# Two-layer cross attention on one core: the row maxima go into the query stack by three transfers of one row each

## The chip, the cores and the metric

The kernel runs on one core of a Trainium2 chip. The metric is the device time of one execution in microseconds (us), given as the median of several runs; before the change it is 413.09 us.

## The reference

Two layers of the same grouped-query cross attention are applied one after the other to `x` (16 batches, 128 rows, 256 columns), each with its own weights and the same context `ctx_2048`:

```python
q = hidden_state @ Wq + bq          # 32 heads of 8
k = encoder_hidden_state @ Wk + bk  # 8 key heads of 8, each for 4 query heads
v = encoder_hidden_state @ Wv + bv
scores = einsum('bkgld,bksd->bkgls', q, k) * 8**-0.5 + mask
attn = softmax(scores, axis=-1)
out = einsum('bkgls,bksd->bkgld', attn, v)   # back to (batch, 128, 256)
x = out @ Wo + bo + hidden_state
return (x - mean(x)) * rsqrt(var(x) + 1e-6) * gamma + beta
```

All values are float32. The mask of these inputs is zero everywhere.

## The kernel before

The work is cut into 32 units (`UNITS`): 16 batches of layer 0 and then 16 of layer 1. Each engine runs a list of phases; phase t holds work of several units at once: scores of unit t, the softmax and the values of units t-1 and t-2, the end of units t-3 and t-4, and the projections of unit t+2. `walk` (L85) writes some phases out one by one and puts the phases 5 to 12 and 21 to 28 into loops of four phases a turn. Within each engine the order is the order of the source; semaphores tie the engines together.

Scores are computed twice. Each float32 query and key is split into three bf16 parts (`PARTS` = 3), and the products of parts stand as rows of two stacks in SBUF: `q_stack` and `k_stack`, four buffers each (`RING`), with rows 0 to 71 for the products of parts (padded with zeros to 96). First `scores` (L655) makes the scores with queries on the partitions, one bank of four heads at a time, and the VectorE takes the maximum of each row (`maximum`, L520). Then `scoresT` (L675) makes them again, transposed, from 99 rows of the stacks: rows 96 to 98 of `q_stack` hold the negated row maxima in three bf16 parts, and the same rows of `k_stack` hold ones, so that the maximum is subtracted inside the matmul and ScalarE can take the exponential at once (L436).

How the maxima get there: after the eighth `maximum` of unit u, `copy_max` (L527) repeats the 32 maxima of each query three times, TensorE transposes them (`transpose_max`, L731 to L740) into 96 partitions, and in the next phase the VectorE splits them with four instructions in `max_rows` (L533; L539, L541, L544, L546) into `max_parts`: partitions 0 to 31 hold the third part of the 32 heads, 32 to 63 the second, 64 to 95 the first, 128 bf16 values (256 bytes) in each partition. `max_parts` has two buffers. The transfer of L290 then copies these 96 rows of 256 bytes into the partitions 96 to 98 of `q_stack`, 32 rows behind each other in each partition. It counts up `max_rows_loaded` by 16. Three places wait on that semaphore: the SyncE queue itself, before it issues the transfer of the next unit (L288); `max_rows` (L538), before it writes over the buffer of two units before; and `scoresT` of the first key head (L678), which is TensorE's to wait for.

In TensorE's list of phase t (L793 to L850), the first `scoresT` of unit t-1 comes after the fifth bank of scores of unit t (L829 to L832). Behind it in the same queue stand the rest of the scores of unit t, the projections and the products with the values.

All transfers are issued by SyncE (L251 to L348), in one queue, in this order in a phase: the maxima of unit t-1 (L290), y of unit t-4 to the result or back to `x_sb` (L298, L301), in layer 0 the inputs of unit t+3 (L258, two) and x of unit t (L312), the query parts of unit t+2 to DRAM (L318), in layer 0 its key parts (L322, three, one for each part), and, when these have landed, the loads of the two stacks of unit t+2 from DRAM (L332 for `q_stack`, L338 for `k_stack`).

Of the kernel before, what the change touches and what calls it, by code (L numbers as in the profile page):

```python
# [37 lines left out]
HEADS, KV, HD = 32, 8, 8  # L38
# [3 lines left out]
PARTS = 3  # L42
TERM_ROWS = PARTS * PARTS * HD
SCORE_ROWS = 96
MAX_ROW = 96
STACK_ROWS = MAX_ROW + PARTS
RING = 4
# [26 lines left out]
def need(engine, sem, count):  # L74

    if not isinstance(count, int) or count > 0:
        engine.wait_ge(sem, count)
# [22 lines left out]
def cross_attention(nc, x, xT, ctxT, mask, w_q, w_kv, w_o, b_q, b_k, rows, out):  # L100
    with ExitStack() as ctx:
        def sb(name, shape, dt):
            return ctx.enter_context(nc.sbuf_tensor(name, shape, dt))
# [36 lines left out]
        q_stack = sb("q_stack", [P, RING, HEADS, L], BF16)  # L140
# [3 lines left out]
        max_parts = sb("max_parts", [PARTS * HEADS, 2, L], BF16)  # L144
# [63 lines left out]
        max_rows_loaded = sem("max_rows_loaded")  # L208
# [19 lines left out]
        MAXT_STEPS, NORM_STEPS, MASK_STEPS = 4, 5, 5  # L228
# [22 lines left out]
        @block.sync  # L251
        def _(sp):
            xT_d = xT.rearrange("(k p) b l -> p k b l", p=P)

            def load_inputs(b, slot, loaded):
                for to, from_ in ((xT_sb[:, :, b], xT_d[:, :, b]),
                                  (ctx_sb[:, slot], ctxT[b].rearrange("(k p) s -> p k s", p=P))):
                    sp.dma_start(to, from_).then_inc(loaded, 16)  # L258


            STARTERS = 2
            sp.dma_start(wq_sb[:, 0], w_q[0].rearrange("(k p) n -> p k n", p=P)).then_inc(weights_loaded, 16)
            load_inputs(0, 0, weights_loaded)
            sp.dma_start(wkv_sb[:].rearrange("p k a n -> p k (a n)"),
                         w_kv.rearrange("(k p) n -> p k n", p=P)).then_inc(weights_loaded, 16)
            sp.dma_start(bq_sb[:], b_q).then_inc(biases_loaded, 16)
            sp.dma_start(bk_sb[:], b_k).then_inc(biases_loaded, 16)
            load_inputs(1, 1, inputs_loaded)
            sp.dma_start(rows_sb[:].rearrange("p a n -> p (a n)"), rows.partition_broadcast(P)).then_inc(rows_loaded, 16)
            sp.dma_start(mask_sb[:], mask.rearrange("b o l s -> l (b o) s")).then_inc(all_masks_loaded, 16)  # L270

            def phase(turn, step, loop_layer):
                t, r = turn + step, step % RING

                def of(per, k):

                    return turn * per + per * (step + k)

                if not isinstance(turn, int):

                    for count in (of(MAXT_STEPS, 0), of(16, -1), of(KV, -RING), of(3, 3), of(1, 0),
                                  of(16 * INPUT_DMAS, 2), of(16, 0), of(2, -3), of(16, -4), of(1, -3),
                                  of(16 * STACK_DMAS, 2), of(16, 3), of(16 * PARTS, 3), of(KV, 3 - RING)):
                        sp.to_reg(count)
                if live(t - 1):

                    need(sp, maxT_step, of(MAXT_STEPS, 0))
                    need(sp, max_rows_loaded, of(16, -1))  # L288
                    need(sp, scoresT_ready, of(KV, -RING))
                    sp.dma_start(q_stack[MAX_ROW:MAX_ROW + PARTS, (r - 1) % RING],  # L290
                                 max_parts[:, (r - 1) % 2].rearrange("p (o l) -> p o l", o=1)).then_inc(max_rows_loaded, 16)
                u, ru = t - 4, r
                if live(u):
                    layer, b = place(u, loop_layer)
                    need(sp, affine_step, of(2, -3))
                    need(sp, y_left, of(16, -4))
                    if layer == LAYERS - 1:
                        sp.dma_start(out[b], y[:, ru % 2]).then_inc(y_left, 16)  # L298
                    else:
                        need(sp, x_bo_ready, of(1, -3))  # L300
                        sp.dma_start(x_sb[:, b], y[:, ru % 2]).then_inc(y_left, 16)  # L301
                layer, b = place(t + 3, loop_layer)
                if (not isinstance(t, int) or t + 3 >= STARTERS) and layer == 0:

                    need(sp, qk_projected, of(1, 0))
                    need(sp, v_projected, of(1, 0))
                    need(sp, inputs_loaded, of(16 * INPUT_DMAS, 2))
                    load_inputs(b, (r + 3) % RING, inputs_loaded)
                layer, b = place(t, loop_layer)
                if live(t) and layer == 0:  # L310
                    need(sp, x_loaded, of(16, 0))
                    sp.dma_start(x_sb[:, b], x[b]).then_inc(x_loaded, 16)  # L312
                u, ru = t + 2, (r + 2) % RING
                layer, b = place(u, loop_layer)
                if live(u):

                    need(sp, q_split, of(3, 3))
                    sp.dma_start(q_scratch[u].rearrange("a p n -> p a n"), q_parts[:, ru % 2]).then_inc(q_stored, 16)  # L318
                    if layer == 0:
                        need(sp, k_split, of(3, 3))  # L320
                        for part in range(PARTS):
                            sp.dma_start(k_scratch[b, :, :, part].rearrange("a d (h s) -> (a d) h s", h=KV),  # L322
                                         k_parts[:, ru % 2, part]).then_inc(k_stored, 16)

                    need(sp, stacks_loaded, of(16 * STACK_DMAS, 2))

                    need(sp, scoresT_ready, of(KV, 3 - RING))
                    if isinstance(u, int) and u < RING:
                        need(sp, k_padded, 1)
                        need(sp, q_padded, u + 1)  # L330
                    need(sp, q_stored, of(16, 3))
                    sp.dma_start(q_stack[0:TERM_ROWS, ru].rearrange("p h l -> p (h l)"),  # L332
                                 q_scratch[u].rearrange("a (d h) n -> (a d) (h n)", d=HD).unsqueeze(1)
                                 .broadcast_to([PARTS * HD, PARTS, HEADS * L])
                                 ).then_inc(stacks_loaded, 16)
                    if layer == 0:
                        need(sp, k_stored, of(16 * PARTS, 3))
                    sp.dma_start(k_stack[0:TERM_ROWS, ru].rearrange("p h l -> p (h l)"),  # L338
                                 k_scratch[b, layer].rearrange("d a n -> (d a) n").partition_broadcast(PARTS)
                                 ).then_inc(stacks_loaded, 16)  # L340
                if isinstance(t, int) and t == 0:
                    sp.dma_start(wo_sb[:], w_o.rearrange("a (k p) n -> p a k n", p=P)).then_inc(later_weights_loaded, 16)
                    sp.dma_start(wq_sb[:, 1], w_q[1].rearrange("(k p) n -> p k n", p=P)).then_inc(later_weights_loaded, 16)

            walk(sp, phase)
            sp.wait_ge(y_left, 16 * UNITS)
            sp.wait_ge(q_stored, 16 * UNITS)
            sp.wait_ge(k_stored, 16 * PARTS * BATCH)  # L348
# [151 lines left out]
        def _(dve):  # L500
# [32 lines left out]
            def max_rows(u, ru):  # L533


                m, parts = misc_bank[0:PARTS * HEADS, 0:L], max_parts[:, ru % 2]
                need(dve, maxT_ready, u + 1)
                need(dve, max_rows_loaded, 16 * (u - 1))  # L538
                nc.vector.tensor_scalar(parts, m, -1.0, None, ALU.mult).then_inc(maxT_step, 1)  # L539
                dve.wait_ge(maxT_step, MAXT_STEPS * u + 1)  # L540
                nc.vector.scalar_tensor_tensor(out=max_rest[:], in0=m, scalar=-1.0, in1=parts,  # L541
                                               op0=ALU.mult, op1=ALU.subtract).then_inc(maxT_step, 1)
                dve.wait_ge(maxT_step, MAXT_STEPS * u + 2)
                nc.vector.tensor_copy(parts[0:2 * HEADS], max_rest[0:2 * HEADS]).then_inc(maxT_step, 1)  # L544
                dve.wait_ge(maxT_step, MAXT_STEPS * u + 3)
                nc.vector.tensor_tensor(parts[0:HEADS], max_rest[0:HEADS], parts[0:HEADS], ALU.subtract  # L546
                                        ).then_inc(maxT_step, 1)
# [106 lines left out]
        def _(pe):  # L654
# [20 lines left out]
            def scoresT(u, ru, kv, masked):  # L675

                if kv == 0:
                    need(pe, max_rows_loaded, 16 * (u + 1))  # L678
                need(pe, exp_done, KV * u + kv - 1)
                mm = nc.tensor.matmul(t_bank[kv % 2][:], k_stack[0:STACK_ROWS, ru, kv],  # L680
                                      q_stack[0:STACK_ROWS, ru, GROUP * kv:GROUP * (kv + 1)],
# [217 lines left out]
```

## Time and profile before

| what | us |
|---|---|
| median of 3 runs | 413.09 |
| the runs | 409.84, 413.18, 413.09 |
| span of the profiled execution | 413.5 |
| TensorE busy | 332.6 |
| VectorE busy | 303.6 |
| GpSimd busy | 249.6 |
| ScalarE busy | 237.1 |

The profiled execution's own time is its span, 413.5 us from its first to its last instruction; it lies 0.4 us above the median of the runs. Busy times are those of the profile; register, semaphore and DMA-issuing instructions are not counted as busy. In the rows below PE is TensorE (PEld its weight loads), DVE VectorE, ACT ScalarE, POOL GpSimd and SPq the queue of SyncE, where the duration of a row is that of the issuing instruction and not of the transfer. Over the whole span the granted clock of TensorE is 0.915 of the full one on average.

### The profile page before, as it was taken

How to read it: one execution, taken by the hardware profiler on the slowest of the kernel's cores; microseconds unless marked ns; L12 is line 12 of the kernel's file. 1: busy time of each engine (PE TensorE's matmuls, PEld its weight loads, DVE VectorE, ACT ScalarE, POOL GpSimd, SP SyncE). 2: the span in 40 equal slices, each digit the busy share in tenths (PEclk: the TensorE clock that was granted, in tenths of full speed). 3: DMA queues.
4: the chain of work that ended last, by engine and by line, in shares of the span. 5: the costliest groups of instructions: out<-in, count | busy, mean ns of one | idle time of the engine just before them, and what ended most of it. 6: DMA issues, size and time to landing. Idle time of an engine off the chain costs nothing.

```text
span 413.5 us, 10069 instructions
## 1 busy us (share of the span) xinstructions
PE 332.6 (80%) x2688; PEld 220.3 (53%) x2688; DVE 303.6 (73%) x796; ACT 237.1 (57%) x530; POOL 249.6 (60%) x505
## 2 busy tenths in 40 slices
PE   3371478898799798979989888988888988888982
PEld 3361355665566564756646555555555655544431
DVE  4432347787669586867969899989989999997832
ACT  2210146677467475756757777766656766654760
POOL 8046505676568576666757766666666766664234
PEclk9855569999889898998989999999999999998997
DMA  7715744544635445453434333333333333331000
GB/s 203 196 35 148 177 112 131 141 131 122 154 88 152 130 131 143 124 151 95 123 108 119 106 109 105 97 116 104 100 113 106 105 110 107 105 93 35 15 29 25
DMA packets 45928, 46.44 MB, mean 112 GB/s; under 512 B 12736, under 2 KB 40640, under 8 KB 43584
## 3 DMA queue, kind: packets, MB, share of 16 engines
q1 hardware_dynamic: 45888, 45.96, 39.8%
q8 instruction: 19, 0.31, 0.3%
q14 instruction: 21, 0.17, 0.1%
HBM read 33.10 MB, written 9.96 MB: 104 GB/s over the span
## 4 chain that ended last, share of the span: by engine, by line
PE 35%; DMA 28%; DVE 18%; issue 11%; POOL 3%; SPq 2%; DVEq 1%; POOLq 0%
DMA q_stack<-max_parts 24%; PE oT_bank L748 9%; PE t_bank L680 8%; PE s_bank L665 8%; DVE row_max L523 5%; PE qk_bank L722 3%; DVE max_parts L546 3%; DVE max_parts L544 3%; PE o_bank L761 2%; DMA mask_sb<-mask 2%; DVE max_rest L541 2%; DMA q_scratch<-q_parts 2%; PE misc_bank L700 2%; DVE max_parts L539 2%; DVE v_ones L603 1%
## 5 line engine op out<-in xcount | busy, mean ns | idle before, releaser
L523 DVE TENSOR_REDUCE row_max<-s_bank 128x4 f32<-128x512 f32 x256 | 171.5, 681 | 68.7 <-PE s_bank L665 67.5
L436 ACT ACTIVATE probs<-t_bank 128x512 f32<-128x512 f32 x256 | 148.7, 602 | 86.7 <-PE t_bank L680 86.5
L680 PE MATMUL t_bank<-q_stack,k_stack 99*128 99x512 bf16 x256 | 102.2, 400 | 44.0 <-DMA q_stack<-max_parts 43.9
L665 PEld LDWEIGHTS s_bank<-k_stack,q_stack 96*128 96x128 bf16 x1024 | 77.4, 103 | 92.2 <-issue 44.5
L665 PE MATMUL s_bank<-k_stack,q_stack 96*128 96x128 bf16 x1024 | 106.2, 230 | 19.7 <-DMA k_stack<-k_scratch 16.5
L748 PE MATMUL oT_bank<-probs,v_ones 128*32 128x512 f32 x512 | 72.7, 642 | 0.2 <-ACT probs L436 0.2
L393 POOL TENSOR_TENSOR scaled<-normed,rows_sb 128x256 f32<-128x256 f32 x32 | 23.2, 726 | 52.8 <-DVE normed L584 52.8
L680 PEld LDWEIGHTS t_bank<-q_stack,k_stack 99*128 99x128 bf16 x256 | 25.7, 101 | 52.2 <-DMA q_stack<-max_parts 44.2
L452 ACT ACTIVATE qT<-qk_bank,bq_scaled 128x128 f32<-128x128 f32 x64 | 23.4, 366 | 49.4 <-PE qk_bank L727 29.3
L441 ACT ACTIVATE oT_sb<-oT_bank 128x512 f32<-128x512 f32 x64 | 39.1, 610 | 18.7 <-PE oT_bank L748 18.7
L236 POOL TENSOR_TENSOR q_rest<-qT,q_parts 128x256 f32<-128x256 f32 x31 | 20.9, 675 | 42.9 <-ACT q_parts L452 33.5
L389 POOL TENSOR_TENSOR rstd<-var_eps,minus_half 128x1 f32<-128x1 f32 x32 | 17.6, 550 | 45.4 <-DVE var_eps L580 44.8
L722 PE MATMUL qk_bank<-xT_sb,wq_sb 128*128 128x128 f32 (+1 forms) x256 | 38.2, 297 | 7.5 <-DMA wkv_sb<-w_kv 6.2
L722 PEld LDWEIGHTS qk_bank<-xT_sb,wq_sb 128*128 128x128 f32 x256 | 37.1, 211 | 9.2 <-issue 7.0
L761 PE MATMUL o_bank<-identf,oT_sb 128*128 128x128 f32 x256 | 39.4, 277 | 1.0 <-ACT oT_sb L441 0.9
L761 PEld LDWEIGHTS o_bank<-identf,oT_sb 128*128 128x128 f32 x256 | 32.1, 144 | 7.9 <-ACT oT_sb L441 2.7
L780 PE MATMUL misc_bank<-wo_sb,attnT 128*128 128x256 f32 x128 | 33.0, 379 | 0.5 <-ACT attnT L466 0.5
L780 PEld LDWEIGHTS misc_bank<-wo_sb,attnT 128*128 128x128 f32 x128 | 24.2, 190 | 3.3 <-ACT attnT L466 0.7
L400 POOL TENSOR_TENSOR y<-scaled,rows_sb 128x256 f32<-128x256 f32 x32 | 23.2, 726 | 3.6 <-POOL scaled L393 1.4
L452 ACT ACTIVATE q_parts<-qk_bank,bq_scaled 128x128 bf16<-128x128 f32 x64 | 23.4, 366 | 0.0
L424 POOL TENSOR_TENSOR x_bo<-x_sb,rows_sb 128x256 f32<-128x256 f32 x32 | 23.4, 731 | 0.0
L239 POOL TENSOR_TENSOR q_parts<-q_rest,q_parts 128x256 bf16<-128x256 f32 x31 | 20.8, 672 | 2.4
(67 smaller groups left out, 432.6 us busy)
## 6 DMA issues: line engine op xcount, KB each, us to landing
q_stack<-q_scratch SPq DMA_DIRECT2D x32, 576.0 KB
q_scratch<-q_parts SPq DMA_DIRECT2D x32, 192.0 KB, 2.5
k_stack<-k_scratch SPq DMA_DIRECT2D x32, 144.0 KB
xT_sb<-xT SPq DMA_DIRECT2D x16, 128.0 KB, 2.8
ctx_sb<-ctxT SPq DMA_DIRECT2D x16, 128.0 KB, 3.4
x_sb<-x SPq DMA_DIRECT2D x16, 128.0 KB, 2.5
x_sb<-y SPq DMA_DIRECT2D x16, 128.0 KB, 2.5
result<-y SPq DMA_DIRECT2D x16, 128.0 KB, 2.3
```

The costliest lines, as they stand in the source:

```text
L393: nc.gpsimd.tensor_tensor(scaled[:], normed[:], rows_sb[:, layer, D:2 * D], ALU.mult).then_inc(affine_step, 1)
L424: nc.gpsimd.tensor_tensor(x_bo[:], x_sb[:, b], rows_sb[:, layer, 0:D], ALU.add).then_inc(x_bo_ready, 1)
L436: nc.scalar.activation(probs[:, ru % 2, kv], t_bank[kv % 2][:], ACT.Exp).then_inc(exp_done, 1)
L441: nc.scalar.activation(oT_sb[:, half], oT_bank[:], ACT.Copy).then_inc(oT_copied, 1)
L452: nc.scalar.activation(q, qk_bank[:, k * L:(k + 1) * L], ACT.Identity, bias=bq_scaled[:, place(u, layer)[0], k:k + 1], scale=SCALE).then_i ...
L523: nc.vector.tensor_reduce(row_max[:, ru % 2, GROUP * kv:GROUP * (kv + 1)], s_bank[kv % 2][:].rearrange("p (g s) -> p g s", g=GROUP), AX.X, ...
L665: mm = nc.tensor.matmul(s_bank[kv % 2][:, g * S:(g + 1) * S], q_stack[0:SCORE_ROWS, ru, GROUP * kv + g], k_stack[0:SCORE_ROWS, ru, kv], st ...
L680: mm = nc.tensor.matmul(t_bank[kv % 2][:], k_stack[0:STACK_ROWS, ru, kv], q_stack[0:STACK_ROWS, ru, GROUP * kv:GROUP * (kv + 1)], start=Tr ...
L722: mm = nc.tensor.matmul(qk_bank[:, n * L:(n + 1) * L], wq_sb[:, layer, k, n * P:(n + 1) * P], xT_sb[:, k, b], start=(n == 0 and k == 0), s ...
L748: mm = nc.tensor.matmul(oT_bank[32 * j:32 * (j + 1)], v_ones[:, ru, kv], probs[:, ru % 2, kv], start=True, stop=True)
L761: mm = nc.tensor.transpose(o_bank[:, g * P:(g + 1) * P], oT_sb[:, half, g * L:(g + 1) * L], identf[:])
L780: mm = nc.tensor.matmul(misc_bank[:, 0:D], attnT[:, k], wo_sb[:, layer, k], start=(k == 0), stop=(k == KT - 1))
```

## The change

The one transfer of L290 becomes three, each from 32 partitions of `max_parts` into one partition of `q_stack`. All three count up the same semaphore, and each count that is waited for becomes three times as large.

```diff
-                    need(sp, max_rows_loaded, of(16, -1))
+                    need(sp, max_rows_loaded, of(16 * PARTS, -1))
                     need(sp, scoresT_ready, of(KV, -RING))
-                    sp.dma_start(q_stack[MAX_ROW:MAX_ROW + PARTS, (r - 1) % RING],
-                                 max_parts[:, (r - 1) % 2].rearrange("p (o l) -> p o l", o=1)).then_inc(max_rows_loaded, 16)
+                    for part in range(PARTS):
+                        sp.dma_start(q_stack[MAX_ROW + part:MAX_ROW + part + 1, (r - 1) % RING],
+                                     max_parts[HEADS * part:HEADS * (part + 1), (r - 1) % 2]).then_inc(max_rows_loaded, 16)
...
-                need(dve, max_rows_loaded, 16 * (u - 1))
+                need(dve, max_rows_loaded, 16 * PARTS * (u - 1))
...
-                    need(pe, max_rows_loaded, 16 * (u + 1))
+                    need(pe, max_rows_loaded, 16 * PARTS * (u + 1))
```

The same factor stands in the list of counts that SyncE puts into registers at the start of each turn of a loop (L281).

## Rows read from the trace of the kernel before

**Rows 1.** The page, part 4: shares of the span in the chain that ended last
```profile
PE 35%; DMA 28%; DVE 18%; issue 11%; POOL 3%; SPq 2%; DVEq 1%; POOLq 0%
```

**Rows 2.** Waits of the whole span, the engines', then SyncE's: us, times, longest
```profile
PE t_bank L680 <- DMA q_stack<-max_parts: 43.9, 28, 6.9
...
SPq L290 <- DVE max_parts L546: 116.3, 31, 7.5
```

**Rows 3.** The chain in order of time, one phase of layer 1: start, us, what
```profile
236.27 0.67 DVE max_parts L546
...
236.96 3.02 DMA q_stack<-max_parts
...
240.03 0.39 PE t_bank L680
...
247.39 3.01 DMA q_stack<-max_parts
```

**Rows 4.** The chain in order of time, other transfers of the maxima
```profile
106.26 5.18 DMA q_stack<-max_parts
...
131.60 4.85 DMA q_stack<-max_parts
145.05 3.42 DMA q_stack<-max_parts
...
179.51 5.51 DMA q_stack<-max_parts
...
279.17 2.83 DMA q_stack<-max_parts
...
372.21 3.87 DMA q_stack<-max_parts
```

**Rows 5.** Timeline of SyncE's queue, a phase of layer 0: start, us of issue
```profile
121.27 0.77 SPq L290 DMA_DIRECT2D q_stack<-max_parts  x1
...
124.91 0.39 SPq L318 DMA_DIRECT2D q_scratch<-q_parts  x1
...
128.95 0.78 SPq L338 DMA_DIRECT2D k_stack<-k_scratch  x1
131.60 0.77 SPq L290 DMA_DIRECT2D q_stack<-max_parts  x1
```

**Rows 6.** The same queue, three issues in a row in an unrolled phase, and layer 1
```profile
87.85 1.89 SPq L322 DMA_DIRECT2D k_scratch<-k_parts  x3
...
241.71 0.74 SPq L338 DMA_DIRECT2D k_stack<-k_scratch  x1
```

**Rows 7.** Issuing instructions by tile: ns least/median/most, first and last start
```profile
L290 SPq DMA_DIRECT2D q_stack<-max_parts x32: 727/760/790, 45.2 to 391.8; - x32
...
L322 SPq DMA_DIRECT2D k_scratch<-k_parts x48: 546/598/1581, 12.4 to 198.6; - x48
...
L312 SPq DMA_DIRECT2D x_sb<-x x16: 354/409/1582, 34.8 to 217.7; - x16
```

**Rows 8.** DMA issues by line: KB each, median us from issue to landing
```profile
x_sb<-y SPq DMA_DIRECT2D x16, 128.0 KB, 2.5
...
k_scratch<-k_parts SPq DMA_DIRECT2D x48, 32.0 KB, 2.0
```

**Rows 9.** Stretches: us, busy by engine, granted clock, share of 16 DMA engines, GB/s
```profile
238.20:238.35 0.15, 0.15 (x4) 0.15 (x2) 0.15 (x1) 0.11 (x1) 0.01 (x1) 1.00 0.00 0
238.35:238.85 0.50, 0.50 (x8) 0.49 (x7) 0.50 (x2) 0.48 (x1) 0.00 (x0) 1.00 0.21 47
...
239.05:239.50 0.45, 0.03 (x1) 0.00 (x0) 0.45 (x5) 0.23 (x1) 0.00 (x0) 1.00 0.88 280
...
156.80:158.20 1.40, 1.40 (x14) 1.20 (x13) 1.27 (x3) 1.40 (x4) 1.32 (x3) 1.00 0.19 69
```

**Rows 10.** Stretches, same columns: behind a late transfer, and layer 1
```profile
111.40:121.20 9.80, 9.71 (x65) 6.15 (x65) 4.93 (x15) 4.64 (x11) 4.49 (x10) 0.68 0.39 105
...
240.00:250.00 10.00, 9.34 (x81) 6.03 (x81) 9.00 (x22) 7.25 (x16) 7.02 (x14) 1.00 0.35 101
```

More of the change, by code:

```diff
@@ L279, in phase @@
                 if not isinstance(turn, int):
-                    for count in (of(MAXT_STEPS, 0), of(16, -1), of(KV, -RING), of(3, 3), of(1, 0),
+                    for count in (of(MAXT_STEPS, 0), of(16 * PARTS, -1), of(KV, -RING), of(3, 3), of(1, 0),
                                   of(16 * INPUT_DMAS, 2), of(16, 0), of(2, -3), of(16, -4), of(1, -3),
```

## The prediction

> **What bounds the kernel now.** I read the chain that ended last first. DMA holds 28% of it [rows 1], and nearly all of that is one transfer, the one that the change cuts up. In order of time the chain has 26 pieces of it that sum to 99.2 us, 24% of the span [rows 3, 4]. A phase of layer 1 shows the loop: VectorE's last split of the maxima (L546) ends at 236.94, the transfer takes 3.02 us, TensorE starts L680 at 240.03, and 7.41 us after the landing the next transfer is issued at 247.39 [rows 3]. Behind the one of 4.85 us issued at 131.60 the same distance is 8.60, up to 145.05 [rows 4]. So a period is the latency of this transfer plus 7.4 us or somewhat more, and a microsecond added to or taken from the latency should come out whole in the time. The waits confirm it from the other side: TensorE waits for this transfer 28 times, 43.9 us in all, and SyncE waits for L546 before it issues 31 times [rows 2]: the queue is nearly always ready before the data.
>
> The latency has two kinds. Of the 26 pieces 13 last over 3.4 us (8.66 for the first unit, then up to 5.51, mostly in layer 0), 13 last 2.83 to 3.28; the six that the chain doesn't hold I count as quiet. So there are 19 quiet ones and 13 held up. What holds them up: the loads of the stacks. In layer 0 the load of `k_stack` is issued 7.68 us after L290 and only 2.65 us before the next L290, whose transfer then takes 4.85 us; in layer 1 it is issued 5.68 us before the next (241.71 to 247.39), which takes 3.01 [rows 3 to 6].
>
> **The quiet latency, term by term.** Only a small part of the 3.02 us is data. Issued at 236.96, the transfer moves nothing up to 238.35 (no DMA work in the stretch before that), then 0.5 us at a share of 0.21, some three of 16 engines, and 47 GB/s x 0.5 us = 24 KB, all of it; a further 1.1 us passes until TensorE goes on [rows 9]. Spreading the data can save at most that half microsecond.
> What is added is issue time. The issue of L290 takes 0.76 us [rows 7]; it is followed by two more. No row shows a 32-row transfer from SBUF into one partition. The nearest for pitch is L322, 128 rows of 256 bytes in a rearranged pattern, three in a row: 1.89 us for three of 0.60, a pitch of (1.89 - 0.60) / 2 = 0.645 us [rows 6, 7]. The lower bound is a plain 0.41 us issue (L312) with 0.05 between, 0.46; the upper is L290's own 0.76 with 0.05, 0.81. I take 0.65, since L322 has the size of row and the reshaping in common.
> From the issue of the last one to its landing: L322 with 32 KB takes 2.0 us, x_sb<-y with 128 KB 2.5 [rows 8]. With 8 KB I take 2.0; the ends are 1.75 (2.0 less half of the data time seen above) and 2.5.
> Latency after: 2 x 0.645 + 2.0 = 3.29 us, against 2.98 as the mean of the quiet pieces now (99.2 less the 60.4 of the held-up ones, over 13): +0.31. From both sides: 2 x 0.46 + 1.75 = 2.67 (-0.31), and 2 x 0.81 + 2.5 = 4.12 (+1.1). 19 x 0.31 = +5.9 us.
>
> **The held-up ones.** Two things pull against each other. Everything behind L290 in SyncE's queue is issued later: three issues of 0.60 and two gaps of 0.05 in place of 0.76 make +1.14 us. In layer 0 the queue runs from L290 to the load of `k_stack` nearly without a gap [rows 5], so that load comes 1.14 us later, and what it still has to move lies that much longer ahead of the next maxima. Against this, the load drains at a share of 0.19, again three engines [rows 9]; if each new transfer is spread over all 16, the three loaded engines have 6 rows of 256 bytes to do behind it in place of 32, which saves about the 0.5 us of data time. The next L290 itself is 0.31 us later by the quiet term. 1.14 - 0.31 - 0.5 = +0.3 a piece. The bounds: +1.1 as for the quiet ones, and -1.0, if the rows now wait behind more than the data time shows. 13 x 0.3 = +3.9 us.
>
> The rest costs nothing while it has cover. The waits of L538 and L288 are for landings of one or two units before, a phase of 10 us away. What the queue delays (y, the inputs, the query parts) is needed a phase or more later. SyncE's last issue ends 1.87 us before the next L290 in a short phase of layer 0 (128.95 + 0.78 to 131.60, register work among it [rows 5]); +1.14 fits, while at the upper pitch +1.6 (3 x 0.76 + 0.10 - 0.76) would leave next to nothing.
>
> Sum: 413.5 + 5.9 + 3.9 = 423.3 us for the profiled execution; the median of the runs is 0.4 below its span, so 422.9, rounded 423.0.
>
> **Two rules of the Trainium skill.** The stretch of 0.5 us shows three engines at work on L290, while x_sb<-y runs at a share of 0.88 [rows 9]. DMA: Bandwidth & Descriptors, in the section on why a DMA increments its semaphore by 16, says that the slowest dimension other than 1 on both sides sets the number of engines; the new shape has 32 on the side of the source in place of 3 against 96, so by that rule all 16 take part. The trace agrees for the old shape. On the other hand the same page's rules for kernel authors say to coalesce many small transfers, since under 64 KB one pays mostly overhead; here 24 KB becomes three times 8 KB. The trace agrees there too: 2.5 of the 3.02 us are not data. By the first rule alone the latency would fall by up to 0.5 us a unit, to about 397 us; by the second it rises.
>
> **The rivals.**
> *Spreading wins (faster).* Place: the landing of L290 behind the load of `k_stack`, on the same three engines. The excess of the 13 held-up ones over 2.98 us is 21.7 us in all. If that excess were mostly these rows being interleaved with other traffic on three engines, then with six rows there it would shrink by two thirds, -14.5 us; with the +5.9 of the quiet ones that gives 404. It decides from a saving of 0.5 us a held-up unit on (5.9 / 13). For it: the second transfer's rows arrive late anyway, so that the added issue time is hidden while the engines drain. Against it: the three engines show 0.19 without a break up to 158.2, which is the load itself, and the new rows wait for that as well, with the load now later. Chance 0.14.
> *It cancels (no change).* A pitch near 0.46 gives 2 x 0.46 + 2.0 = 2.92 quiet, much as now, and the held-up ones gain and lose alike: 413. For it: plain issues take 0.41 us. Against it: these patterns aren't plain, and L290's takes 0.76. Chance 0.13.
> *The issue is dear, or the clock goes (slower still).* At a pitch of 0.81 and 2.2 us to land the quiet latency is 3.8: 19 x 0.82 + 13 x 0.5 = +22, 435 us. Close to it: TensorE waits some 1.1 us a phase in layer 1 at a granted clock of 1.00 (2.4 GHz); behind the transfer of 5.18 us the clock is 0.68 on average, a mix of that level and 1.2 GHz, and the next issue comes 9.8 us after the landing in place of 7.4 (106.26 + 5.18 to 121.27) [rows 4, 5, 10]. Two or three more phases like this are within the range; one in each phase would be more. Chance 0.2.
> My forecast has the rest, 0.53.
>
> **How the numbers follow.** 423.0 us is the likeliest case, with 417 to 430 as its own range (pitch 0.55 to 0.72). The range of all goes from 407, where quiet ones stay and the held-up ones gain 0.5 us each, to 436. About 1% is what a measurement of this kernel can tell from no change. Faster by over 1% is the first rival: 0.14; within 1% the second and a little of the forecast: 0.15; slower: 0.71.
>
> **What would show it.** Right: three issues in a row at a pitch of 0.6 to 0.7 us in SyncE's timeline, quiet pieces of the chain from the first issue to TensorE's start of 3.2 to 3.4 us, a distance from the landing to the next issue still at 7.4, the load of `k_stack` some 1.1 us later behind L290, and held-up ones of 4 to 5.5 us as before. Wrong: chain pieces under 2.9 us in layer 1 (then issue or landing is cheaper than its nearest rows), held-up pieces gone or below 3.6 (then the three engines were the brake), or a period that doesn't follow the latency.

## The result, and the profile after

| | before | after |
|---|---|---|
| median of the runs, us | 413.13 (4 runs, 409.84 to 413.76) | 422.96 (4 runs, 420.10 to 425.33) |
| span of the profiled execution, us | 413.5 | 421.4 |
| ratio after to before | | 1.027, 95% interval 1.0195 to 1.0345 |

The change makes the kernel slower: the medians differ by 9.8 us, 2.4%, and the ratio above, which is formed from the runs and not from the medians, says 2.7%. Executions over 1.5% longer than the fastest of their kernel are left out of every ratio and interval in this document, but not out of the medians. 423.0 was forecast, with 417 to 430 as the likeliest case's own range.

First the chain that ended last, after, as shares of the span. It answers to [rows 1].

```profile
PE 33%; DMA 22%; DVE 19%; issue 11%; SPq 11%; POOL 3%; DVEq 1%; POOLq 0%
```

SyncE's queue, 2% of the chain before, now holds 11%, and DMA went from 28% to 22%. The same piece of work is the brake, but a part of it is now issue time. One phase of layer 1 in order of time (start us, us, what), which answers to [rows 3]:

```profile
250.08 0.67 DVE max_parts L547
...
250.76 0.57 SPq L291
...
251.37 0.59 SPq L291
...
252.00 1.92 DMA q_stack<-max_parts
...
253.96 0.39 PE t_bank L681
...
261.33 0.57 SPq L291
```

The first issue comes right behind VectorE's last split, the second 0.61 us later, the third at 252.00, 1.24 us behind the first, and 1.92 us later all has landed. That is 3.16 us in place of 3.02 in the phase of [rows 3], and from the landing at 253.92 to the next issue at 261.33 it is 7.41 us, exactly the distance of before. The page's table of issues and the tile's durations give the two terms over all 96 transfers (KB each and median us to landing; then ns least/median/most):

```profile
q_stack<-max_parts SPq DMA_DIRECT2D x96, 8.0 KB, 2.0
...
L291 SPq DMA_DIRECT2D q_stack<-max_parts x96: 502/587/1531, 44.3 to 400.0; - x96
```

The held-up transfers are still there. Of this chain, pieces that begin with the third issue; the timeline of SyncE beside them shows the queue of one phase of layer 0, which answers to [rows 5]:

```profile
146.45 3.74 DMA q_stack<-max_parts
...
170.68 3.65 DMA q_stack<-max_parts
...
197.01 2.88 DMA q_stack<-max_parts
```

```profile
121.84 1.86 SPq L291 DMA_DIRECT2D q_stack<-max_parts  x3
...
131.31 0.78 SPq L339 DMA_DIRECT2D k_stack<-k_scratch  x1
133.08 2.81 SPq L291 DMA_DIRECT2D q_stack<-max_parts  x3
```

The load of `k_stack` goes out 9.47 us behind the first issue of the maxima, where it was 7.68: 1.8 us later, of which 1.1 are the two added issues; the rest are short waits in between. Over the phases of layer 0 the median of that distance is 8.6 in place of 7.5, just those 1.1. It stands 1.77 us in front of the next maxima, where it was 2.65. In the last row the three issues take 2.81 us in place of 1.86; that is taken up below.

How many engines take part can be read from the number of packets on the page (before, then after):

```profile
q1 hardware_dynamic: 45888, 45.96, 39.8%
```

```profile
q1 hardware_dynamic: 47328, 45.96, 39.0%
```

1440 more for 32 units is 45 a unit. In the trace's DMA records of this queue only the packets of 4 bytes became more, from 3392 to 4832. I read them as the packets with which each engine that takes part counts up the semaphore. Then they rose from 3 to 48 a unit, if the old transfer used three engines (its share of 0.21 in [rows 9] says so), 16 for each new one. The trace's updates of `max_rows_loaded` bear it out: after, DMA updated it 1536 times, 16 times for each of the 96 transfers.

**Where the 7.9 us between the two profiled executions come from.** I take a unit's latency from its first issue to its last landing, and the rest of the period up to the next first issue. In both executions 19 of the 32 are quiet (below 3.4 us) and 13 held up.

| term, us | before | after | difference |
|---|---|---|---|
| up to the first issue | 45.2 | 44.3 | -1.0 |
| 19 quiet latencies | 56.6 | 60.0 | +3.4 |
| 13 held-up latencies | 60.5 | 62.4 | +1.9 |
| from landing to next issue, 31 times | 232.6 | 235.2 | +2.7 |
| behind the last landing | 18.6 | 19.5 | +0.9 |

The fourth row is no constant. Behind a late landing TensorE has stood idle and its granted clock is lower for a while, as the rows below show; the distance was over 8 us five times before and is so seven times after. One stretch behind a late landing and one behind a quiet one, after (columns as in [rows 9]); they answer to [rows 10]:

```profile
174.40:184.20 9.80, 9.80 (x65) 6.27 (x65) 4.90 (x14) 4.60 (x10) 4.50 (x10) 0.67 0.46 125
208.00:217.00 9.00, 8.95 (x85) 6.09 (x81) 8.15 (x23) 7.10 (x17) 5.76 (x11) 1.00 0.27 86
```

In the first the granted clock is 0.67 on average, a mix of the two levels 2.4 and 1.2 GHz, and the next issue comes 10.0 us behind the landing in place of 7.4.

### The profile page after: what moved, and what is told of

It is laid out like the page before. It is cut to its first block, busy times and chain, and to the rows that moved or that the text cites. A ratio compares the mean times of both kernels' runs of the same rounds, so it can differ in the third digit from the quotient of the medians.

```text
span 421.4 us, 10139 instructions
## 1 busy us (share of the span) xinstructions
PE 333.2 (79%) x2688; PEld 219.6 (52%) x2688; DVE 303.0 (72%) x796; ACT 237.2 (56%) x530; POOL 250.1 (59%) x505
## 4 chain that ended last, share of the span: by engine, by line
PE 33%; DMA 22%; DVE 19%; issue 11%; SPq 11%; POOL 3%; DVEq 1%; POOLq 0%
DMA q_stack<-max_parts 18%; SPq L291 9%; PE t_bank L681 8%; PE oT_bank L749 8%; PE s_bank L666 7%; PE qk_bank L723 4%; DVE row_max L524 4%; DVE max_parts L547 3%; DVE max_parts L545 3%; DVE max_rest L542 2%; DMA mask_sb<-mask 2%; PE o_bank L762 2%; DVE max_parts L540 2%; PE misc_bank L701 2%; DMA ctx_sb<-ctxT 1%
## 5 line engine op out<-in xcount | busy, mean ns | idle before, releaser
L681 PE MATMUL t_bank<-q_stack,k_stack 99*128 99x512 bf16 x256 | 103.1, 404 | 48.3 <-DMA q_stack<-max_parts 48.1
L442 ACT ACTIVATE oT_sb<-oT_bank 128x512 f32<-128x512 f32 x64 | 39.1, 611 | 19.1 <-PE oT_bank L749 19.1
L781 PE MATMUL misc_bank<-wo_sb,attnT 128*128 128x256 f32 x128 | 33.9, 387 | 0.5 <-ACT attnT L467 0.5
```

What stands on the lines that cost most here:

```text
L442: nc.scalar.activation(oT_sb[:, half], oT_bank[:], ACT.Copy).then_inc(oT_copied, 1)
L781: mm = nc.tensor.matmul(misc_bank[:, 0:D], attnT[:, k], wo_sb[:, layer, k], start=(k == 0), stop=(k == KT - 1))
```

## The experiments

The theory: a unit's latency is the pitch of the issues in front of the last one plus the last one's landing, and a second loss comes through SyncE's queue, because what stands behind the maxima in it, the load of `k_stack` above all, goes out later and then holds up the next maxima. The rivals: the number of transfers or their spread over all engines costs something by itself; or the loss is only one of the two terms. In the table, "layer 0" is the time from the first issue of the maxima of unit 0 to that of unit 16, "layer 1" from unit 16 to unit 31, both in the profiled execution.

| kernel | median us | before beside it | ratio (95%) | layer 0 | layer 1 |
|---|---|---|---|---|---|
| before | 413.13 | | | 191.7 | 154.8 |
| after | 422.96 | 413.13 | 1.027 (1.0195 to 1.0345) | 195.9 | 158.6 |
| e1_staged | 403.47 | 412.17 | 0.980 (0.973 to 0.987) | 186.0 | 149.3 |
| e2_two | 416.28 | 412.17 | 1.008 (1.004 to 1.0125) | | |
| e3_extra | 436.01 | 412.17 | 1.063 (1.055 to 1.072) | 202.2 | 161.2 |
| e4_kspread | 401.81 | 412.17 | 0.976 (0.969 to 0.983) | 182.1 | 151.9 |
| e5_after_kspread | 413.97 | 410.72 | 1.007 (1.001 to 1.013) | 188.1 | 154.6 |
| e6_staged_kspread | 389.08 | 410.72 | 0.950 (0.9405 to 0.960) | 176.3 | 147.4 |
| e7_staged_two_kspread | 392.12 | 410.72 | 0.959 (0.952 to 0.9665) | 182.6 | 142.4 |
| e8_x_once | 395.60 | 410.44 | 0.9595 (0.949 to 0.970) | | |
| e9_after_x_once | 415.58 | 410.44 | 1.0135 (1.005 to 1.022) | | |

The kernel before was run again beside each group of kernels, and its own median lay between 410.4 and 413.1 us; kernels of different rows are best set against each other by their ratios. The profiled executions of e2, e8 and e9 were the longest of their kernels (421.4, 397.4 and 421.5 us), so their stretches are left out. That of e5 was the shortest of its ten (408.5 us) and that of e3 the shortest of its four (432.5 us).

### e1_staged: each transfer as soon as its part is split

```diff
-                    need(sp, maxT_step, of(MAXT_STEPS, 0))
...
-                    for part in range(PARTS):
+                    for part, left in ((2, 3), (1, 1), (0, 0)):
+                        need(sp, maxT_step, of(MAXT_STEPS, 0) - left)
```

(Left out: the list of the counts that SyncE puts into registers.)

> Three transfers as in the change, but each issued as soon as its own part is split: the first part after L539, the second after L544, the third after L546. Theory (latency = pitch of the issues + landing of the last one; the engines and the number of transfers cost nothing by themselves): only one issue and one landing lie behind L546, 1.92 us in place of 3.16, so quiet periods fall from 10.57 to the 9.3 to 9.6 us at which VectorE is full; held-up ones stay. Time 395 to 403 us. Rival (what costs is the number of transfers, their wide spread over the engines and the semaphore counts): no less than 418 us, the latency behind L546 stays near 3 us.

403.5 us, 19.5 below the change and 8.7 below the kernel before, with the same 96 transfers over the same 16 engines. The rival falls: three wide transfers are not slow by themselves, what counts is how much of them stands behind the last split. The time lies just above what was expected (395 to 403), and the landing is the likely reason. The tile's summary line (least/median/most of all landings, from each issue) of e1:

```profile
DMA to landing us min/median/max: 1.8/2.4/6.8
```

and of the changed kernel:

```profile
DMA to landing us min/median/max: 1.8/2.0/6.5
```

The median landing is 2.4 in place of 2.0. As the periods shrink, the load of `k_stack` lies nearer to the next maxima, also in layer 1: it is issued 2.9 us before them in the median there, where it was 4.6 in the changed kernel. The expectation that "held-up ones stay" was too simple, more transfers of the maxima became held up. That this load does it here too fits the rows, but no run shows it by itself. TensorE still waits 33.4 us in all for the maxima, against 48.1 after and 43.9 before.

### e2_two: two transfers in place of three

```diff
-                    for part in range(PARTS):
-                        sp.dma_start(q_stack[MAX_ROW + part:MAX_ROW + part + 1, (r - 1) % RING],
-                                     max_parts[HEADS * part:HEADS * (part + 1), (r - 1) % 2]).then_inc(max_rows_loaded, 16)
+                    for first, last in ((1, 3), (0, 1)):
+                        sp.dma_start(q_stack[MAX_ROW + first:MAX_ROW + last, (r - 1) % RING],
+                                     max_parts[HEADS * first:HEADS * last, (r - 1) % 2].rearrange("p (o l) -> p o l", o=1)
+                                     ).then_inc(max_rows_loaded, 16)
```

(Against the changed kernel; the counts, 32 in place of 48, follow and are left out.)

> Two transfers in place of three: 64 rows into two partitions, then 32 rows into one. Theory (pitch + landing of the last): the second is issued 0.65 to 0.8 us after the first and lands 1.92 us later, 2.6 to 2.75; the first, on two engines with 32 rows each, lands about as the transfer of before, 2.8 to 2.9, so that quiet latencies are 2.85, as before, and the time is 411 to 415 us. Rival (each transfer more costs its share, half of what the change cost): 418 us.

416.3 us, between the two. The time alone can't tell them apart: the interval of its ratio puts it 1.7 to 5.2 us above the kernel before, and half of the change's price is 4.9. Its chain in layer 1 has the quiet latency that the theory gave:

```profile
338.49 0.70 SPq L291
339.24 2.06 DMA q_stack<-max_parts
```

2.81 us from the first issue to the landing, no more than before. So the 3 to 4 us that are left are not in the quiet latency. They fit a queue that is 0.6 us longer (issues of 0.70 and 0.59 in place of 0.76), the term that my expectation for this kernel had left out; that they come from there is argued and not shown. In the profiled execution the 19 quiet latencies sum to 54.3 us (before 56.6) and the 13 held-up ones to 66.2 (before 60.5), which has the sign of that reading, but it is the longest execution of ten.

### e3_extra: the queue made longer, the transfer of the maxima left alone

```diff
+                    need(sp, spare_loaded, of(32, -1))
+                    for n in range(2):
+                        sp.dma_start(spare[MAX_ROW + n:MAX_ROW + n + 1], ident[HEADS * n:HEADS * (n + 1)]
+                                     ).then_inc(spare_loaded, 16)
```

(Left out: the tile `spare` and its semaphore, a wait for `ident` at the start of SyncE's list and one for the last of these transfers at its end.)

> The kernel before with its one transfer, and behind it in SyncE's queue two more of 8 KB for which nobody in the phase waits (from a constant into a spare tile, same shape as in the change; this is work beyond the reference's). Theory (the second term of the prediction: what is queued behind goes out 1.25 us later, so the load of k_stack holds up the next maxima for longer): quiet latencies stay at 2.8 to 3.0 us, the held-up ones of layer 0 grow by 0.6 to 1.2 us each, time 419 to 426 us. Rival (the queue behind L290 has room, all of the loss is the pitch in front of the last landing): 411 to 415 us.

436.0 us, +24, where 419 to 426 was expected: the direction is the theory's, the size is twice its. Nobody in a phase waits for these two transfers, yet they cost more than the whole change. The chain shows both kinds of latency grown, held-up ones in layer 0 and now also in layer 1:

```profile
121.53 6.13 DMA q_stack<-max_parts
146.96 6.40 DMA q_stack<-max_parts
...
302.11 4.54 DMA q_stack<-max_parts
...
335.72 3.21 DMA q_stack<-max_parts
346.43 3.16 DMA q_stack<-max_parts
```

Over its 32 units the latencies sum to 133.9 us, against 117.1 before and 122.4 after. Sixteen are held up, by 5.17 us on average (before 13, 4.65; after 13, 4.80), and the quiet ones are mostly at 3.16, 0.2 to 0.3 above before, which I had not expected. That part is not the theory's: 0.32 us more (3.16 against 2.84) in each of 32 units would be some 10 of the 16.8 us by which the latencies grew (an estimate), and a quiet unit is one that the load of `k_stack` doesn't hold up. Only the other 6.6 us or so are left for that load.

Set beside the change this is the most telling run. The load of `k_stack` goes out equally late behind the first issue, 9.50 us here and 9.47 there:

```profile
121.53 0.76 SPq L292 DMA_DIRECT2D q_stack<-max_parts  x1
...
131.03 0.78 SPq L344 DMA_DIRECT2D k_stack<-k_scratch  x1
```

But here the maxima travel as one transfer on three engines and there as three on sixteen. The change is 13 us faster than e3. A quiet unit takes 3.16 us in both, so the 11.5 us between the two sums of latencies (133.9 and 122.4) lie with the held-up ones: the narrow transfer suffers more from what runs beside it. How e3's +24 us divides between the later load and the two extra transfers, which also carry data, isn't shown; for that a run would have to lengthen the queue without adding a transfer.

### e4_kspread: the load of k_stack in three transfers

```diff
-                    sp.dma_start(k_stack[0:TERM_ROWS, ru].rearrange("p h l -> p (h l)"),
-                                 k_scratch[b, layer].rearrange("d a n -> (d a) n").partition_broadcast(PARTS)
-                                 ).then_inc(stacks_loaded, 16)
+                    for n in range(PARTS):
+                        sp.dma_start(k_stack[TERM_ROWS // PARTS * n:TERM_ROWS // PARTS * (n + 1), ru].rearrange("p h l -> p (h l)"),
+                                     k_scratch[b, layer].rearrange("d a n -> (d a) n")).then_inc(stacks_loaded, 16)
```

(with `STACK_DMAS = 4`)

> The kernel before, with the load of k_stack made of three transfers of 24 rows each, which by the shape can use twelve engines in place of three. Theory (what holds the maxima up is this load on the three engines that also carry them): its data drain in about a fourth of the time, the held-up latencies fall from 3.4 to 5.5 us to below 3.5 in most units although SyncE issues 1.3 us more per phase, time 396 to 405 us. Rival (what holds them up is SyncE's late issue or the traffic of all loads together): held-up latencies stay above 4 us in layer 0, time 410 to 420 us.

401.8 us, as expected, and the rival falls: only six latencies are over 3.4 us, in place of 13. The same kind of edit as the change, one transfer made three, here wins 10 us. Its packets and its issues show why:

```profile
q1 hardware_dynamic: 46944, 45.96, 43.1%
```

```profile
L339 SPq DMA_DIRECT2D k_stack<-k_scratch x96: 313/356/1348, 16.7 to 354.4; - x96
```

1056 packets more are 33 a unit, from 3 to 36: twelve engines for each transfer. And the three issues take 0.36 us each, 1.2 us together, against 0.75 for the one: the split costs the queue only 0.45 us, not the 1.3 that was expected. A quiet landing stays at 2.87 in layer 1.

### e5_after_kspread: the change on top of e4

> The changed kernel with the load of k_stack in three transfers of 24 rows, as in e4_kspread; to be set against e4_kspread (401.8 us). With the held-up latencies mostly gone, the change's own price is left. Theory (pitch in front of the last landing, and room in SyncE's queue): quiet latencies 3.15 us in place of 2.87 in layer 1, +0.3 a unit, and in layer 0 the queue, which was busy for some 9.4 us a phase, is busy for 10.5 and begins to set the period: 409 to 415 us. Rival (what the change cost came only through the load of k_stack on three engines): 401 to 404 us, as e4_kspread.

414.0 us, 12.2 above e4_kspread; the rival falls. The size is less certain than the sign: the ten runs lie between 408.5 and 417.9 us, but even the lowest is above all four of e4 (at most 402.3), and by the two ratios to the kernel before, 1.007 and 0.976, the change costs 3% here. The price of the change is not tied to the slow load: with it mended, quiet latencies in layer 1 are 3.13 in place of 2.87, and eleven latencies are over 3.4 us again, in place of six, ten of them in layer 0; all latencies sum to 117.2 us, against 107.0 in e4. The room in SyncE's queue has shrunk as well:

```profile
SPq L291 <- DVE max_parts L547: 76.2, 29, 6.7
```

SyncE waits 76 us in all for the last split, where it waited 100 in the changed kernel and 116 before [rows 2].

### e6_staged_kspread and e7_staged_two_kspread: both together

e6 has the edits of e1 and of e4; e7 sends 64 rows after L544 (of the kernel before) and 32 after L546.

> Both at once: each of the three transfers as soon as its part is split (e1_staged), and the load of k_stack in three (e4_kspread). Theory (the two took different things away: the pitch and a part of the landing from in front of TensorE, and the drain of three engines): the gains add where SyncE has room. Layer 1: latency behind the last split 1.92 us and periods of 9.3 to 9.6, VectorE full; layer 0: SyncE is busy for some 10.5 us a phase and sets the period. Time 385 to 394 us. Rival (one of the two gains only moved the wait, so that they don't add): 398 to 403 us.

> As e6_staged_kspread, but with two transfers of the maxima: 64 rows into two partitions after L544, and the last 32 rows after L546. One issue less per phase, 0.6 us. Theory (in layer 0 SyncE's queue is the bound): layer 0 gains up to 0.6 us a phase against e6_staged_kspread, layer 1 loses 0.1 to 0.3 us a phase because 64 rows on two engines land 2.85 us after L544: 383 to 392 us, within 4 us of e6_staged_kspread. Rival (the queue isn't the bound): slower than e6_staged_kspread by 3 us or more.

e6 takes 389.1 us, 5.0% below the kernel before: the gains add (8.7 + 10.4 = 19.1 expected from e1 and e4, 21.6 measured). This version beats both the kernel before and the change. e7 is 3.0 us slower, at the point where its expectation drew the line, so it tells little: in layer 0, where it has one issue less, it is slower (182.6 against 176.3), in layer 1 faster (142.4 against 147.4), the opposite of what I had reckoned. That SyncE's issues alone bound layer 0 of e6 is thus not borne out.

### e8_x_once and e9_after_x_once: one issue less in layer 0

```diff
-                    need(sp, x_loaded, of(16, 0))
-                    sp.dma_start(x_sb[:, b], x[b]).then_inc(x_loaded, 16)
...
+                    sp.dma_start(x_sb[:], x.rearrange("b p d -> p b d")).then_inc(x_loaded, 16)
```

(The new line stands in phase 0; GpSimd's wait for x, left out, becomes one for 16.) e8 is e6 with this edit, e9 the changed kernel with it.

> As e6_staged_kspread, and the 16 loads of x in layer 0 are made one load of 2 MB in phase 0: SyncE issues one transfer less in each phase of layer 0, with its register work 0.55 us. Theory (in layer 0 SyncE's queue sets the period, or how late the load of k_stack goes out): layer 0 gains 0.3 to 0.55 us a phase, 5 to 8 us, against 389.1 us, less what the 2 MB cost at the start: 381 to 387 us. Rival (the queue has room, and layer 0 is bound by its transfers): 388 to 392 us.

> The changed kernel with the same one load of x: its queue in layer 0 is shorter by 0.55 us a phase, half of the 1.04 us that the change added (1.86 in place of 0.77 and the gap). Theory (the length of the queue in front of the load of k_stack is a large part of the loss, as e3_extra said): the load goes out 0.5 us earlier and the held-up latencies of layer 0 fall by 0.3 to 0.5 us: 415 to 420 us. Rival (the pitch in front of the landing is all): 422 to 424 us.

e8 missed: 395.6 us, 6.5 above e6 and outside what theory and rival gave. e9 came out as the theory has it: 415.6 us, 7.4 below the change, though only 4.7 when each is set against the kernel before beside it (+5.1 and +9.8), and the intervals of the two ratios overlap. In the trace of each the load of all of x delays the start, the first issue of the maxima comes at 47.6 us (e6: 42.2) and at 50.1 (after: 44.3). Behind that point e9's trace is 7.4 us shorter in layer 0, where the queue has half a microsecond less per phase, and 0.7 longer in layer 1, where it has the same. e8's trace is only 2.0 us shorter than e6's in layer 0, which doesn't pay for the start, and 4.5 longer in layer 1, which no edit explains; the traces of e8 and e9 are each of the longest execution. In e8 the load of `k_stack` is spread, in e9 not, and one could read from this that a long queue is dear only while it pushes a load on three engines against the maxima. That is not shown, and e5 speaks against it: there the load is spread as well, and the longer queue with the later landing still cost 3%.

## Why the prediction was right, by its own steps

**What bounds the kernel: right.** That a microsecond of latency comes out whole is shown in the chain after (7.41 us again between landing and next issue) and by e3's trace: its latencies sum to 16.8 us more than before, the distances from landing to next issue to the same 232.6, and its span is 17.1 us longer. e1, which takes time from behind the last split, gets 19.5 us back against the change. Behind late landings more than the latency is lost, see below.

**The pitch: right.** 0.645 was taken from L322; it is 0.62, issues of 0.587 us and a gap of 0.03 to 0.04. Neither the plain issue of 0.41 nor the old one of 0.76 would have done.

**The landing: right, slightly too long.** 2.0 was taken, 1.92 measured. Latency after: 3.29 forecast, 3.16 measured; against 2.98 that is +0.18 a quiet unit and +3.4 us in all, where the sum had +5.9.

**The held-up ones: the net has the right sign, its terms are not confirmed.** +3.9 forecast, +1.9 in the two traces. It is the difference of two terms of opposite sign. What spreading gives back, put at 0.5 us a held-up unit or 6.5 us in all, is larger: against e3, with the queue equally long and the quiet latency the same, the held-up units of the change have 11.5 us less. The queue term, +1.14 - 0.31 a unit or +10.8 in all, stands in no run by itself. e3's +24 us is more than it, but the two transfers also made every quiet landing later, which the term doesn't hold. A third term, the late issues and landings beside instruction packets (last section), was not foreseen and holds up to some 5 us of the 62.4.

So the near hit of 423.0 is in part luck, and a reader should take it for less than it looks. In the traces the two terms of the sum came to +5.3 us in place of +9.8, and terms that weren't in the sum brought the difference up to 7.9. The likeliest case's own range was also not what its words say: with the rest of the sum worked out in the same way, pitches of 0.55 and 0.72 give some 418 and 427, not 417 and 430.

**The distance from landing to next issue: left out of the sum.** It was named in the third rival (two or three more phases behind a lower clock "are within the range"); the traces have two more such phases, and +2.7 us.

**From the profiled execution to the median: wrong in form.** I set the execution's own time equal to its span, 0.4 us above the median. Later runs list both numbers, for instance 423.27 us with a span of 421.4, so 1.9 us lie around the span. The profiled execution of before thus took an estimated 415.4 us, and was 2 us slower than its median; its own time is not on record. That accounts for the 1.9 us between the traces' difference of 7.9 and the medians' of 9.8; executions of one kernel differ by 4 to 5 us here.

**The rivals.** "Spreading wins" had a true mechanism, as e4 and the change beside e3 show, but not the size to turn the sign. "It cancels" asked for a pitch of 0.46. "The issue is dear, or the clock goes" was half there: the issue wasn't dear, the clock went twice more.

**The two rules of the Trainium skill.** The rule on the number of engines in DMA: Bandwidth & Descriptors, in the section on why a DMA increments its semaphore by 16, gave the right counts: by the packets 3 before and 16 after, and 12 for e4's 24 rows. As a forecast of the time it would by itself have had the wrong sign here and the right one for e4. The same page's rule for kernel authors to coalesce many small transfers would have had the right sign here and the wrong one for e4.

Which way a split goes could be estimated from the rows: whether the data time on few engines (0.5 us for 24 KB; some 2 us for the load of 144 KB at the 69 GB/s of its stretch [rows 9]) is larger than the issues that the split adds.

## What to carry to other kernels

Cut a transfer into several only where its data time on few engines is longer than the added issues, or where the parts are ready at different times and each can leave at once; on the way to a waiting engine, what was issued before the last producer was done came nearly free here (e1). When SyncE issues everything in one queue, cost each added transfer also by what it pushes towards the next critical one, and by what it does beside the critical one: two transfers a phase that nobody waited for cost 24 us here, in shares that stay open. And look at the outermost dimension of the transfers that run beside the critical one: an ordinary-looking broadcast load on three engines cost 10 us (e4).

## What the runs showed of the hardware that I had not expected

**Issues that hang for a microsecond.** Four issues of the maxima take 1.37 to 1.53 us after, in place of 0.59. None of the maxima's did before, when the longest was 0.79, though one of L322 and one of L312 took 1.58 [rows 7]. In the chain:

```profile
133.08 0.60 SPq L291
...
133.72 1.53 SPq L291
...
135.30 2.38 DMA q_stack<-max_parts
```

Two units of layer 1, which the table above counts with the held-up ones (4.10 and 4.11 us), land a microsecond late without a long issue of their own. Here is one of them, behind an ordinary unit:

```profile
283.79 1.92 DMA q_stack<-max_parts
...
294.46 2.85 DMA q_stack<-max_parts
```

and the next issue in the queue takes 1.17 us in place of 0.4:

```profile
295.31 1.17 SPq L299 DMA_DIRECT2D result<-y  x1
```

All six stand beside a packet of the instruction queue. In the trace's DMA records a packet of 16,384 bytes lasts 0.98 us from 86.1 on, 1.36 from 133.5, 1.25 from 195.3, 1.22 from 218.7, 1.08 from 295.0 and 1.21 from 370.5; the long issues begin at 86.1, 133.7, 195.5, 218.9, 295.3 and 370.7. The long issue of L322 in the trace before (1.58 us at 100.5) stands beside such a packet too (100.4). The page before has 19 of these packets, as many as after:

```profile
q8 instruction: 19, 0.31, 0.3%
```

The likely reading is that a transfer on all sixteen engines, in a queue that is busy with the maxima for 1.86 us a phase in place of 0.76, meets such a packet more often than one on three. For it: an issue of the maxima takes over 1 us three or four times in the trace of each kernel with three transfers on sixteen engines (after, e1, e5, e6, e8, e9), and never in the others. Against the width alone: e2 and e7 have one such transfer a phase and e3 has two, and none of these issues hangs (the longest of e3's 64 takes 0.84 us). It was not tried by itself. The six together hold up to some 5 us of latency; how much of that the kernel before pays in other units stays open.

**The time of an issue goes by the shape more than by the bytes.** One load of `k_stack` on three engines (144 KB) takes 0.75 us to issue, about as long as the three rows of maxima (24 KB, 0.76); a third of it on twelve engines 0.36; one row of maxima 0.59, two rows 0.70.

**Transfers that follow can make the one in front land later.** In e3, with two transfers issued behind it, the quiet landing of an unchanged transfer went from 2.84 to 3.16 us in the steady part of layer 1. What in the engines does this stays open.
